# The first 128 tokens of one expert, gathered early and multiplied in float32, in a two-layer kernel with a mixture of experts

## The chip, the core and the metric

The kernel runs on one core of a Trainium2 chip, as one program with one instruction stream for each engine: PE (TensorE), DVE (VectorE), ACT (ScalarE), POOL (GpSimd) and SP (SyncE, which only starts DMAs here). The metric is device time in microseconds of one execution; the kernel before takes 1387.16 us, the median of three runs (1385.14 to 1389.26 us).

## The reference

x is (32, 64, 1024) in float32, seen as N = 2048 rows ("tokens") of 1024. There are two layers, and the change touches the second alone:

```python
x = x + L0_ffn(L0_cond(x))          # a grouped convolution, then an NF4 feed-forward with LoRA
# L1_cond: an 8-fold mixture of 64x64 kernels over the channels of each batch element
att = softmax(gelu(gelu(emb @ W0 + b0) @ W1 + b1) @ W2 + b2)
z = einsum('boi,bih->boh', einsum('bk,koi->boi', att, weight), x) + (att @ bias_k)[:, :, None]
# L1_ffn: each token goes to one of 8 experts
sel = argmax(softmax(z @ gate_w.T + gate_b))
for j in range(8):
    out = out + where(sel == j, z @ expert_w[j].T + expert_b[j], 0)
x = x + out
```

The gate's argmax decides which weights (1024 x 1024 floats an expert) a token meets. Worked out from the reference's inputs, the experts get 788, 125, 536, 196, 99, 180, 56 and 68 of the 2048 tokens, and expert 0 gets 391 of the first 1024.

## The kernel before, in words

**The first layer** takes the first 1045 us or so. It ends with the accumulators `acc` (16 tiles of 128 tokens) in SBUF.

**The mixing stage** runs over those 16 tiles (the loop at L1587). For tile t, PE mixes channels (`mixed`, L1514), ACT copies the sums out of PSUM as z32 (`mixed_out`, L757), PE transposes them (`z_transposed`, L1524), ACT copies the turned tile (`z_copied`), PE multiplies by the gate (`gate`, L1534), DVE adds the gate's bias (`logit`, L1081), PE turns the eight logits to rows (`pick_out`, L1546) and DVE copies them (`picked`). POOL stores each tile's z rows to HBM in two DMAs (L515), and SP loads expert 0's weights one eighth (`kt`, 512 KB) at a time as tiles finish (`load_expert`, L432). An SP wait on `z_ready` sets when each eighth may go.

**Placing.** The tokens are sorted by expert in tiles of 128 with no host help. `choose` makes one-hot rows of the argmax. `ranks` (PE, L1550) counts, for each token, the tokens before it that chose the same expert. `places` and `digits` (DVE) turn rank and expert into a slot. `marked` (DVE, L1132) makes two indicator rows for each tile of tokens, and `placed` (PE, L1567) multiplies them into one table in PSUM that holds at each slot the token's number. This is done in three batches of tiles, `BATCHES = (0, 6, 11, 16)`. After the last one, DVE turns the sums into `table` (L1198), then works out which expert and which column of the table each of the NS = 23 output tiles has (`etf`, `columns`, `through`, `side`, `loads`, L1201 to L1224). In the meantime PE has nothing to multiply and runs dummy products (`spin`, L1287).

**The expert stage** is 23 tiles, always all of them. For tile s:

- POOL's queue, written out by hand in `tile` (L564), gathers z rows by the table three tiles ahead (`gather_z`), gathers x rows two ahead (`gather_x`), adds the expert's bias to the x rows by a DMA one ahead (`add_bias`, semaphore `xb_in`) and scatters the finished tile.
- PE transposes the gathered z rows (`rows_transposed`, L1614, issued inside the tile before), and multiplies: 8 values of kt, two halves of 512 columns, three products each (`three`, L1279: high x high, high x low, low x high of a split of float32 in two float32r parts), so 48 products of 128 x 512.
- ACT makes the high parts (`convert_high`, with `z_high`), DVE the low parts (`convert_low`, with `z_low`), from the raw weights `wraw` for every tile anew. There is one copy of the split weights (`whr`, `wlr`), so that kt of the next tile is converted once PE has done kt of this one.
- DVE adds the product to the x rows (`add_rows`, L1246), at the end of the conversion of the next tile, and waits for `xb_in` before it.

The first tile has its own code: `first_high` on ACT (all eight high parts, then the turned z in halves), `first_low` on DVE, and `rows_transposed(0, 0)` and five more `spin` products on PE.

Of the kernel before, what the change touches and what calls it, by code (L numbers as in the profile page):

```python
# [48 lines left out]
BATCHES = (0, 6, 11, TILES)  # L49
# [41 lines left out]
def program(nc, x_nat, x_conv, toep, cond_t, ctx_w_t, chan_bias, codes_up, codes_dn, am_up, am_dn, bias_up,  # L91
# [5 lines left out]
    with ctx:  # L97
# [3 lines left out]
        def sb(stack, name, shape, dt=F32):  # L101
# [134 lines left out]
        columns = sb(moe, "columns", [P, NSP], I32)  # L236
# [3 lines left out]
        eti = sb(moe, "eti", [P, NSP], I32)  # L240
        side = sb(moe, "side", [P, NSP], I32)
        sidef = sb(moe, "sidef", [P, NSP])
        loaded = sb(moe, "loaded", [P, 2, NSP])
        loads = sb(moe, "loads", [P, 2, NSP], I32)
# [3 lines left out]
        xidx = sb(moe, "xidx", [P, 4], I32)  # L248
        xg = sb(moe, "xg", [P, 4, L])
        zg = sb(moe, "zg", [P, 4, L])  # L250
# [34 lines left out]
            "iotas", "route_const", "route_dve", "chosen", "seen_ready", "rank_mm", "total_mm", "row_ready", "slot_mm"))  # L285
        table_ready, columns_ready, tiles_ready = sem("table_ready"), sem("columns_ready"), sem("tiles_ready")
        half_turned, half_high, half_low = sem("half_turned"), sem("half_high"), sem("half_low")
# [17 lines left out]
        def gate_bank(t):  # L305
            return bank[{TILES - 3: 0, TILES - 2: 1, TILES - 1: 4}.get(t, 6)]
# [18 lines left out]
        def _(sp):  # L325
# [118 lines left out]

            for kt in range(KT):
                sp.sem_inc(wraw_in[1][kt], 16)
            load_expert(0)
            load_expert(1)
# [6 lines left out]
        def _(pool):  # L455
            last_row = pool.to_reg(N - 1)
# [55 lines left out]
            for t in range(TILES):  # L512
                pool.wait_ge(z_ready, 2 * (t + 1))
# [10 lines left out]
            def gather_z(i, s):  # L524
# [4 lines left out]
                if isinstance(i, int) and 4 * i + s == 0:  # L529
                    rows = table[:, 0:1]  # L530
# [60 lines left out]
        def _(act):  # L591
# [190 lines left out]
            def first_high():  # L782

                for kt in range(KT):
                    act.wait_ge(wraw_in[0][kt], 16)
                    nc.scalar.activation(whr[:, kt], wraw[:, 0, kt], ACT.Copy).then_inc(whr_ready, 1)
                both = pair[2][:].rearrange("p (k s) -> p k s", k=KT)
                act.wait_ge(half_turned, 1)
                nc.scalar.activation(zth[:, 0, 0:KT // 2], both[:, 0:KT // 2], ACT.Copy).then_inc(half_high, 1)
                act.wait_ge(tr_mm, 1)  # L790
                nc.scalar.activation(zth[:, 0, KT // 2:], both[:, KT // 2:], ACT.Copy).then_inc(zth_ready, 1)
# [22 lines left out]
            first_high()  # L814
            act.wait_ge(tiles_ready, TABLES)
            for i in rounds(act, NS // 4):
                for s in range(4):
                    if not (isinstance(i, int) and i == s == 0):
# [5 lines left out]
        def _(dve):  # L824
# [289 lines left out]

            def places(b):
# [8 lines left out]
            def digits(b):  # L1124
                a, z = BATCHES[b:b + 2]
                link(nc.vector.tensor_copy(sloti[:, 0, a:z], slotf[:, a:z]))
                nc.vector.tensor_single_scalar(sloti[:, 1, a:z], sloti[:, 0, a:z], P - 1, ALU.bitwise_and).then_inc(route_dve, 1)
                step[0] += 1
# [9 lines left out]
            for t in range(TILES):  # L1138
# [4 lines left out]
                if t == TILES - 1:  # L1143
                    marked(6, 7)
# [11 lines left out]
                elif t == 2:  # L1156
                    nc.vector.tensor_scalar(far[:], iota_f[:, 0:E], float(N), None, ALU.mult).then_inc(route_const, 1)
# [8 lines left out]
                elif t == 7:  # L1166
                    choose(0)
                elif t == 8:
                    places(0)
                    digits(0)  # L1170
                elif t == 9:
                    count_seen(0)
                    marked(0, 2)
                elif t in (10, 11):
                    marked(2 * t - 18, 2 * t - 16)
                elif t == 12:
                    choose(1)
                    count_seen(1)
                elif t == 13:
                    places(1)  # L1180
                elif t == 14:
                    digits(1)
            logit(TILES - 1)
            picked(TILES - 2)
            marked(7, 8)
# [4 lines left out]
            digits(2)  # L1190
            marked(10, TILES)

            dve.wait_ge(total_mm, 1)
            link(nc.vector.tensor_tensor(more[:], by_entry(bank[1][:, 0:E], TILES),
                                         room[:].rearrange("p (o e) -> p o e", o=1).broadcast_to([P, E, TILES]), ALU.is_gt))
# [13 lines left out]
            link(nc.vector.scalar_tensor_tensor(out=columnf[:], in0=etf[:], scalar=float(TILES), in1=iota_f[:, 0:NSP],  # L1209
                                                op0=ALU.mult, op1=ALU.add))  # L1210
            link(nc.vector.tensor_tensor(columnf[:], columnf[:], begin[:], ALU.subtract))
            nc.vector.tensor_copy(columns[:], columnf[:]).then_inc(columns_ready, 1)
            nc.vector.tensor_scalar(through[:], start[:], float(KT), 1.0, ALU.mult, ALU.add).then_inc(tiles_ready, 1)
            nc.vector.tensor_copy(eti[:], etf[:]).then_inc(tiles_ready, 1)
            dve.wait_ge(tiles_ready, 2)
            nc.vector.tensor_single_scalar(side[:], eti[:], 1, ALU.bitwise_and).then_inc(tiles_ready, 1)
            dve.wait_ge(tiles_ready, 3)
            nc.vector.tensor_copy(sidef[:], side[:]).then_inc(tiles_ready, 1)
# [4 lines left out]
            for b in range(2):  # L1223
                nc.vector.tensor_scalar(loads[:, b], loaded[:, b], 8.0, 16.0, ALU.mult, ALU.add).then_inc(tiles_ready, 1)  # L1224

            def first_low():
                both = pair[2][:].rearrange("p (k s) -> p k s", k=KT)
                for kt in range(KT):
                    dve.wait_ge(whr_ready, kt + 1)
                    nc.vector.tensor_tensor(wlr[:, kt], wraw[:, 0, kt], whr[:, kt], ALU.subtract).then_inc(wlr_ready, 1)  # L1230
                    if kt == 1:
                        for h in range(2):
                            k = slice(h * KT // 2, (h + 1) * KT // 2)
                            if h == 0:
                                dve.wait_ge(half_high, 1)
                            else:
                                dve.wait_ge(zth_ready, 1)
                            nc.vector.tensor_tensor(ztl[:, 0, k], both[:, k], zth[:, 0, k],
                                                    ALU.subtract).then_inc(ztl_ready if h else half_low, 1)
# [5 lines left out]

            def add_rows(i, s):  # L1246
                wait(dve, chunk_mm, i * 32 + KT * (s + 1))
                dve.wait_ge(xb_in[s % 4], i * 16 + 16 * (s // 4 + 1))
                nc.vector.tensor_tensor(xg[:, s % 4], xg[:, s % 4], pair[s % 2][:], ALU.add).then_inc(y_ready, 1)
# [14 lines left out]
            dve.sem_inc(wlr_ready, KT)  # L1264
            first_low()
            dve.wait_ge(tiles_ready, TABLES)
            for i in rounds(dve, NS // 4):
                for s in range(4):
                    if not (isinstance(i, int) and i == s == 0):
# [6 lines left out]
        def _(pe):  # L1276
# [257 lines left out]
            def gate(t):  # L1534
                pe.wait_ge(zt_high, t + 1)
                wait(pe, zt_ready, t + 1 - HALVED)
                if t < TILES - 3:
                    wait(pe, lt_ready, t)
                    wait(pe, logit_ready, t)
# [27 lines left out]
            def placed(first, last):  # L1567
                for t in range(first, last):
                    pe.wait_ge(row_ready, 2 * (t + 1))
                    ins = mm(bank[7][:, P:P + SC], atrow[:, t], atcol[:, t], start=t == 0, stop=t == TILES - 1)  # L1570
                if last == TILES:
                    ins.then_inc(slot_mm, 1)
# [14 lines left out]
            for t in range(TILES + 2):  # L1587
                if t < TILES:
                    z_transposed(t)
                if 1 < t < TILES:  # L1590
# [5 lines left out]
                elif t == 8:  # L1596
                    ranks(0)
                elif t == 13:
                    ranks(1)
# [12 lines left out]
            pe.wait_ge(table_ready, 1)  # L1612
# [9 lines left out]

            def product(i, s):
                first = isinstance(i, int) and i == s == 0
                if first:
                    pe.wait_ge(half_low, 1)
                else:
                    pe.wait_ge(ztl_ready, i * 4 + s + 1)

                wait(pe, y_ready, i * 4 + s - 1)  # L1630
                for kt in range(KT):
                    if first and kt == KT // 2:
                        pe.wait_ge(ztl_ready, 1)
                    pe.wait_ge(wlr_ready, i * 32 + KT * (s + 1) + kt + 1)
                    for h in range(2):
                        d = slice(h * 512, (h + 1) * 512)
                        ins = three(bank[2 * (s % 2) + h], zth[:, s % 2, kt], ztl[:, s % 2, kt], whr[:, kt, d],
# [6 lines left out]
            spin(bank[1], 5)  # L1644
            for i in rounds(pe, NS // 4):
                for s in range(4):
                    product(i, s)
# [69 lines left out]
```

## Time and profile before

| | us |
|---|---|
| three runs, median (lowest to highest) | 1387.16 (1385.14 to 1389.26) |
| the profiled execution's own time | 1384.71 |
| its span in the trace | 1383.1 |
| mixing stage, first `mixed` to last `gate` | 1045.2 to 1090.8 |
| first expert product starts | 1106.51 |
| last `add_rows` starts | 1378.3 |

The span is what the trace shows between the first and the last instruction; the execution's own time has 1.6 us around it. PE is busy for 99% of the span, but its spins count as busy. DVE is busy for 81% of the span, and for nearly all of the expert stage. Times below are from the span's start.

### The profile page before, as it was taken

How to read it: one execution, taken by the hardware profiler on the slowest of the kernel's cores; microseconds unless marked ns; L12 is line 12 of the kernel's file. 1: busy time of each engine (PE TensorE's matmuls, PEld its weight loads, DVE VectorE, ACT ScalarE, POOL GpSimd, SP SyncE). 2: the span in 40 equal slices, each digit the busy share in tenths (PEclk: the TensorE clock that was granted, in tenths of full speed). 3: DMA queues.
4: the chain of work that ended last, by engine and by line, in shares of the span. 5: the costliest groups of instructions: out<-in, count | busy, mean ns of one | idle time of the engine just before them, and what ended most of it. 6: DMA issues, size and time to landing. Idle time of an engine off the chain costs nothing.

```text
span 1383.1 us, 20668 instructions
## 1 busy us (share of the span) xinstructions
PE 1369.2 (99%) x6816; PEld 1125.6 (81%) x6816; DVE 1113.5 (81%) x1127; ACT 774.5 (56%) x872; POOL 225.6 (16%) x251
## 2 busy tenths in 40 slices
PE   9999999999999999999999999999999899999998
PEld 8987888888888888888888888888765688888887
DVE  7879887878878788787887887878643799999997
ACT  6665554545454545445464554555216677777774
POOL 0120000001000000000000000000013256645653
PEclk9999999999999999999999999999999999999999
DMA  7863756587874779666886759885588786978952
GB/s 243 343 248 137 270 205 244 188 290 250 276 272 176 273 252 288 238 241 225 282 250 245 261 195 298 255 286 214 198 303 283 238 256 153 375 198 290 352 173 54
DMA packets 105108, 339.50 MB, mean 245 GB/s; under 512 B 15716, under 2 KB 23404, under 8 KB 105036
## 3 DMA queue, kind: packets, MB, share of 16 engines
q1 hardware_dynamic: 79122, 257.93, 50.1%
q0 software_dynamic: 25376, 80.24, 21.5%
q8 instruction: 36, 0.59, 0.2%
q10 hardware_dynamic: 546, 0.50, 0.1%
q14 instruction: 28, 0.23, 0.0%
HBM read 303.49 MB, written 46.14 MB: 253 GB/s over the span
## 4 chain that ended last, share of the span: by engine, by line
PE 94%; DVE 3%; issue 1%; ACT 1%; DMA 0%; POOL 0%; DVEq 0%; SPq 0%; ACTq 0%; POOLq 0%
PE pair L1281 27%; PE pair L1282 27%; PE pair L1283 27%; PE pair L1350 4%; PE pair L1618 1%; DVE wf L873 1%; PE pair L1530 1%; PE pair L1520 1%; PE pair L1464 1%; PE pair L1382 1%; PE pair L1365 1%; PE pair L1542 1%; PE pair L1343 1%; PE pair L1290 1%; PE pair L1419 0%
## 5 line engine op out<-in xcount | busy, mean ns | idle before, releaser
L873 DVE TENSOR_TENSOR wf<-wf,term 128x1024 f32<-128x1024 f32 x308 | 376.5, 1222 | 62.7 <-ACT term L618 48.3
L618 ACT ACTIVATE term<-codes 128x1024 f32<-128x1024 int32 x308 | 320.6, 1055 | 137.7 <-DVE wf L873 137.7
L1281 PE MATMUL pair<-wh,hh 128*128 128x512 f32 x672 | 263.3, 392 | 1.6 <-DVE acc L937 1.3
L1282 PE MATMUL pair<-wl,hh 128*128 128x512 f32 x672 | 262.0, 390 | 0.0
L1283 PE MATMUL pair<-wh,hl 128*128 128x512 f32 x672 | 262.0, 390 | 0.0
L1281 PE MATMUL pair<-ring,wh 128*128 128x512 f32 x624 | 242.9, 389 | 0.0
L1282 PE MATMUL pair<-ring,wh 128*128 128x512 f32 x624 | 242.9, 389 | 0.0
L1283 PE MATMUL pair<-ring,wl 128*128 128x512 f32 x624 | 242.7, 389 | 0.0
L943 DVE TENSOR_TENSOR acc<-acc,pair 128x1024 f32<-128x1024 f32 x160 | 194.5, 1216 | 46.2 <-PE pair L1283 40.2
L807 ACT ACTIVATE whr<-wraw 128x1024 fp32r x176 | 181.1, 1057 | 63.9 <-PE pair L1283 49.8
L1255 DVE TENSOR_TENSOR wlr<-wraw,whr 128x1024 fp32r<-128x1024 f32 x176 | 203.4, 1215 | 2.1 <-ACT whr L807 1.9
L1281 PEld LDWEIGHTS pair<-wh,hh 128*128 128x128 f32 x672 | 126.2, 188 | 31.3 <-issue 2.9
L1283 PEld LDWEIGHTS pair<-wh,hl 128*128 128x128 f32 x672 | 126.1, 188 | 26.6
L1282 PEld LDWEIGHTS pair<-wl,hh 128*128 128x128 f32 x672 | 126.2, 188 | 25.9
L1281 PE MATMUL pair<-whr,zth 128*128 128x512 f32 x368 | 145.4, 395 | 0.9 <-DVE ztl L1243 0.9
L1283 PE MATMUL pair<-whr,ztl 128*128 128x512 f32 x368 | 143.5, 390 | 0.0
L1282 PE MATMUL pair<-wlr,zth 128*128 128x512 f32 x368 | 143.4, 390 | 0.0
L647 ACT ACTIVATE wh<-wf 128x1024 fp32r<-128x1024 f32 x44 | 45.6, 1058 | 174.6 <-DVE wf L892 159.8
L1283 PEld LDWEIGHTS pair<-ring,wl 128*128 128x128 f32 x624 | 117.1, 188 | 24.4
L1281 PEld LDWEIGHTS pair<-ring,wh 128*128 128x128 f32 x624 | 117.2, 188 | 24.1
L1282 PEld LDWEIGHTS pair<-ring,wh 128*128 128x128 f32 x624 | 117.2, 188 | 23.9
L489 POOL DMA_DIRECT2D acc<-x_nat x16 | 13.9, 867 | 678.7 <-DVE acc L943 678.7
(202 smaller groups left out, 1557.3 us busy)
## 6 DMA issues: line engine op xcount, KB each, us to landing
ring<-x_parts SPq DMA_DIRECT2D x320, 512.0 KB, 6.5
wraw<-exp_w SPq DMA_DIRECT2D x64, 512.0 KB, 10.5
x_parts<-stage POOLq DMA_DIRECT2D x24, 512.0 KB, 7.0
xg<-exp_b POOLq DMA_DIRECT2D x23, 512.0 KB, 7.9
codes<-codes_up SPq DMA_DIRECT2D x22, 512.0 KB, 7.1
codes<-codes_dn SPq DMA_DIRECT2D x22, 512.0 KB, 6.8
am<-am_dn SPq DMA_DIRECT2D x22, 512.0 KB, 4.1
acc<-x_nat POOLq DMA_DIRECT2D x16, 512.0 KB, 5.5
```

Of the source, the lines that this page charges most:

```text
L489: pool.dma_start(acc[:, bass.ds(i + (CT * c - 1), 1)].rearrange("p a l -> p (a l)"), x_nat[bass.ds(i * P + (CT * c - 1) * P, P)], accum_op ...
L618: return nc.scalar.activation(out, codes[:, n % 2], ACT.Relu, scale=scale, bias=-scale * bend)
L647: nc.scalar.activation(high_part(n), whole(n), ACT.Copy).then_inc(wh_ready, 1)
L807: nc.scalar.activation(whr[:, kt], wraw[:, bass.ds(buf, 1), kt].rearrange("p a n -> p (a n)"), ACT.Copy).then_inc(whr_ready, 1)
L873: nc.vector.tensor_tensor(whole(n), whole(n), term[:, e % 2], op).then_inc(term_added, 1)
L943: nc.vector.tensor_tensor(a, a, pair[2 + j % 2][:], ALU.add).then_inc(acc_added, 1)
L1255: nc.vector.tensor_tensor(wlr[:, kt], wraw[:, bass.ds(buf, 1), kt].rearrange("p a n -> p (a n)"), whr[:, kt], ALU.subtract).then_inc(wlr_r ...
L1281: mm(ps, ah, bh, start=first, stop=False)
L1282: mm(ps, ah, bl, start=False, stop=False)
L1283: return mm(ps, al, bh, start=False, stop=last)
L1290: mm(ps[:, 0:blocks * P].rearrange("p (c n) -> p c n", n=P), ones[:].bitcast(F32R), ones[:].bitcast(F32R).rearrange("p (o n) -> p o n", o= ...
L1350: ins = mm(whole_bank[:, :, g * GC:(g + 1) * GC], xcv[h][p % 4][:, k % 2, g, d:d + P], tz[h][:, d, g], start=k == g == d == 0, stop=k > 0 ...
```

## The change

The first eight tiles of tokens (1024 of them) become batch 0 of the placing. As soon as they are counted, the kernel picks the expert with the most of them (`fullest`), loads that expert's weights a second time into the other weight buffer, and makes the expert's first 128 tokens an output tile of their own, tile 0 (the "lead"). Their rows come from a table that only the first eight tiles went into. The lead is multiplied from plain float32 weights and plain float32 turned rows, with no split: 16 products instead of 48. The placing of the remaining tiles, the last batch's ranks included, follows in PE's order behind the lead's transposes and inside the lead's product. The 22 other tiles follow as before, with one tile fewer for that expert. All `spin` products of this stage are gone.

```diff
-BATCHES = (0, 6, 11, TILES)
+BATCHES = (0, TILES // 2, 11, TILES)
@@ SP
-                        sp.wait_ge(z_ready, 2 * TILES if e else 4 * kt + 2)
+                        sp.wait_ge(*((chunk_mm, kt + 1) if e else (z_ready, min(4 * kt + 2, 26))))
+            def load_lead():
+                sp.wait_ge(lead_ready, 1)
+                first = sp.value_load(eti[0:1, 0:1], min_val=0, max_val=E - 1)
+                for kt in range(KT):
+                    sp.dma_start(wraw[:, 1, kt], exp_w[bass.ds(first, 1), :, kt].rearrange("a p n -> p (a n)")
+                                 ).then_inc(wraw_in[1][kt], 16)
             load_expert(0)
+            load_lead()
             load_expert(1)
@@ POOL
             for t in range(TILES):
+                if t == TILES - 1:
+                    for k in range(ZB):
+                        pool.wait_ge(z_stored[k], 32 * (TILES // 2) // ZB)
+                    pool.wait_ge(lead_rows_ready, 1)
+                    pool.indirect_dma_start(zg[:, 0], None, z_dram[0:N // 2], bass.IndirectOffsetOnAxis(lead_rows[:], 0), ...
                 pool.wait_ge(z_ready, 2 * (t + 1))
...
-            gather_z(0, 0)
+            gather_z(0, 1)
             pool.wait_ge(columns_ready, 1)
-            for s in range(1, 3):
-                gather_z(0, s)
+            gather_z(0, 2)
             gather_x(0, 0)
             gather_x(0, 1)
@@ ACT
-            first_high()
+            first_high(0, 2)
+            lead_turned()
+            first_high(2, KT)
+            z_high(0, 1)
@@ DVE
+            def lead():
+                counts = bank[7][:, 3 * P:3 * P + E]
+                dve.wait_ge(count_mm, 1)
+                link(nc.vector.reduce_max(most[:], counts, AX.X))
+                link(nc.vector.tensor_scalar(fullest[:], counts, most[:, 0:1], None, ALU.is_equal))
+                link(nc.vector.tensor_tensor(fullest[:], fullest[:], rising[:], ALU.mult))
+                link(nc.vector.reduce_max(mark[:], fullest[:], AX.X))
+                ... (three scalars of mark: eti[0], columns[0], leadf; then taken and far)
+            def rows_of_lead():
+                dve.wait_ge(lead_mm, 1)
+                link(nc.vector.tensor_tensor(lead_column[:], bank[7][:, 2 * P:2 * P + SC], lead_column[:], ALU.mult))
+                link(nc.vector.reduce_sum(leadf[:], lead_column[:], AX.X))
+                nc.vector.tensor_scalar(lead_rows[:], leadf[:], 1.0, -1.0, ALU.mult, ALU.add).then_inc(lead_rows_ready, 1)
             def first_low():
                 for kt in range(KT):
-                    dve.wait_ge(whr_ready, kt + 1)
+                    dve.wait_ge(whr_ready, KT + kt + 1)
                     nc.vector.tensor_tensor(wlr[:, kt], wraw[:, 0, kt], whr[:, kt], ALU.subtract).then_inc(wlr_ready, 1)
+                    if kt == 3:
+                        z_low(0, 1)
+                add_rows(0, 0)
@@ PE
             for t in range(TILES + 2):
+                if t == 10:
+                    ranks(0)
+                    counted()
...
+                if t == 13:
+                    ranks(1)
+                    placed(0, TILES // 2, 2 * P, TILES // 2)
...
-            placed(0, 8)
-            spin(bank[5], 1)
-            ranks(2)
-            totals(1)
-            spin(bank[5], 2)
-            placed(8, TILES)
-            spin(bank[5], 20)
-            pe.wait_ge(table_ready, 1)
+            def lead_product():
+                for kt in range(KT):
+                    if kt == 0:
+                        pe.wait_ge(half_copied, 1)
+                    elif kt == KT // 2:
+                        pe.wait_ge(zth_ready, 1)
+                    pe.wait_ge(wraw_in[1][kt], 16)
+                    for h in range(2):
+                        ins = mm(bank[2 + h], lead_turn[:, kt], wraw[:, 1, kt, h * 512:(h + 1) * 512],
+                                 start=kt == 0, stop=kt == KT - 1)
+                    ins.then_inc(chunk_mm, 1)
+                    if kt == 1:
+                        placed(TILES // 2, TILES)
+                    elif kt == 5:
+                        pe.wait_ge(table_ready, 1)
+                        rows_transposed(0, 1)
             rows_transposed(0, 0)
-            spin(bank[1], 5)
+            placed(0, TILES // 2)
+            ranks(2)
+            totals(1)
+            lead_product()
```

DVE's calls are moved within the loop over t: `choose(0)` and `count_seen(0)` from t = 7 and 9 to t = 9, `lead()` and `places(0)` at t = 10, `digits` and `marked(0, 2)` and `(2, 4)` at t = 11, `choose(1)`, `lead_columns()` and `marked(4, 6)` at t = 12, `marked(6, 8)` and `rows_of_lead()` at t = 13, `places(1)` at t = 14, `digits(1)` at t = 15. The gate of the last tile uses the shared PSUM bank, and `pair` halves of the expert stage swap parity.

## Rows read from the trace of the kernel before

**Rows 1.** Page, part 4: the chain that ended last, by engine.

```profile
PE 94%; DVE 3%; issue 1%; ACT 1%; DMA 0%; POOL 0%; DVEq 0%; SPq 0%; ACTq 0%; POOLq 0%
```

**Rows 2.** Windows: stretch, its us, busy by engine, PEclk, DMA share, GB/s.

```profile
1075.00:1080.00 5.00, 5.00 (x59) 3.14 (x60) 2.62 (x13) 3.90 (x6) 2.35 (x4) 1.00 0.94 306
1098.00:1100.00 2.00, 2.00 (x6) 1.61 (x6) 1.62 (x7) 0.00 (x0) 0.09 (x1) 0.50 0.03 12
1102.00:1104.00 2.00, 2.00 (x10) 1.61 (x10) 1.90 (x7) 0.00 (x0) 0.36 (x2) 1.00 0.63 231
```

**Rows 3.** Timeline of PE around the placing: start, us, engine, line, operation.

```profile
1085.59 0.65 PE L1542 MATMUL pair<-zt,gts 128*32 128x128 f32 x16
1091.67 0.61 PE L1570 MATMUL pair<-atcol,atrow 128*128 128x128 f16 x8
1106.51 0.49 PE L1281 MATMUL pair<-whr,zth 128*128 128x512 f32 x1
1118.44 0.50 PE L1281 MATMUL pair<-whr,zth 128*128 128x512 f32 x1
```

**Rows 4.** Chain of waits in the expert stage: the transposes inside two tiles.

```profile
1121.46 0.87 PE pair L1618 x8
1133.23 0.87 PE pair L1618 x8
```

**Rows 5.** Waits of the expert stage with PE as the waiting engine, all of them.

```profile
PE pair L1281 <- DVE ztl L1243: 0.9, 1, 0.9
```

**Rows 6.** Timeline of DVE.

```profile
1093.98 0.19 DVE L1119 TENSOR_TENSOR place<-pair,far 128x40 f32<-128x40 f32 x1
1098.54 0.29 DVE L1198 SCALAR_TENSOR_TENSOR table<-pair,empty 128x128 int32<-128x128 f32 x1
1102.73 2.35 DVE L1230 TENSOR_TENSOR wlr<-wraw,whr 128x1024 fp32r<-128x1024 f32 x2
1123.98 1.21 DVE L1249 TENSOR_TENSOR xg<-xg,pair 128x1024 f32<-128x1024 f32 x1
1125.11 3.48 DVE L1255 TENSOR_TENSOR wlr<-wraw,whr 128x1024 fp32r<-128x1024 f32 x3
```

**Rows 7.** Timeline of POOL behind the table.

```profile
1099.91 1.12 POOL L537 DMA_INDIRECT zg<-z_rows,table  x1 [11.68 <-issue]
1103.82 1.05 POOL L537 DMA_INDIRECT zg<-z_rows,zidx  x1 [0.96 <-POOL zidx L534]
1105.91 1.02 POOL L537 DMA_INDIRECT zg<-z_rows,zidx  x1 [0.79 <-POOL zidx L534]
1109.00 1.20 POOL L548 DMA_INDIRECT xg<-x_rows,xidx  x1 [0.79 <-POOL xidx L545]
1117.76 1.00 POOL L555 DMA_DIRECT2D xg<-exp_b  x1 [4.15 <-DMA xg<-x_rows,xidx]
```

**Rows 8.** DMA issues, one stretch each, from 1088 to 1128: KB, us to landing.

```profile
z_rows<-z POOLq DMA_DIRECT2D x1, 256.0 KB, 8.5
zg<-z_rows,table POOLq DMA_INDIRECT x1, 4.4
xg<-x_rows,xidx POOLq DMA_INDIRECT x1, 8.0
xg<-exp_b POOLq DMA_DIRECT2D x1, 512.0 KB, 5.3
xg<-x_rows,xidx POOLq DMA_INDIRECT x1, 4.4
xg<-exp_b POOLq DMA_DIRECT2D x1, 512.0 KB, 7.6
wraw<-exp_w SPq DMA_DIRECT2D x16, 512.0 KB, 6.2
```

**Rows 9.** Timeline of PE in the convolution: plain float32 products, two records each.

```profile
85.00 1.95 PE L1350 MATMUL pair<-tz,late_xcv 128*128 128x128 f32 x16
86.71 0.48 PE L1343 MATMUL pair<-ctxd,ones 128*128 128x512 f32 x1
```

More of the change, by code:

```diff
@@ L235, in program @@
         columnf = sb(moe, "columnf", [P, NSP])
-        columns = sb(moe, "columns", [P, NSP], I32)
+        columns = sb(moe, "columns", [P, NSP + 1], I32)
         past = sb(moe, "past", [P, NSP, E])
         etf = sb(moe, "etf", [P, NSP])
-        eti = sb(moe, "eti", [P, NSP], I32)
-        side = sb(moe, "side", [P, NSP], I32)
+        eti = sb(moe, "eti", [P, NSP + 1], I32)
+        side = sb(moe, "side", [P, NSP + 1], I32)
         sidef = sb(moe, "sidef", [P, NSP])
         loaded = sb(moe, "loaded", [P, 2, NSP])
-        loads = sb(moe, "loads", [P, 2, NSP], I32)
+        loads = sb(moe, "loads", [P, 2, NSP + 1], I32)
+        most = sb(moe, "most", [P, 1])
+        fullest = sb(moe, "fullest", [P, E])
+        mark = sb(moe, "mark", [P, 1])
+        taken = sb(moe, "taken", [P, E])
+        leadf = sb(moe, "leadf", [P, 1])
+        lead_column = sb(moe, "lead_column", [P, SC])
+        lead_rows = sb(moe, "lead_rows", [P, 1], I32)
+        free = sb(moe, "free", [P, E, TILES])
         through = sb(moe, "through", [P, E], I32)
@@ L528, in gather_z @@
                 rows = zidx[:, s % 4:s % 4 + 1]
-                if isinstance(i, int) and 4 * i + s == 0:
-                    rows = table[:, 0:1]
+                if isinstance(i, int) and 4 * i + s == 1:
+                    rows = table[:, 1:2]
                     pool.sem_inc(zidx_ready, 1)
@@ L817, in _ @@
                 for s in range(4):
-                    if not (isinstance(i, int) and i == s == 0):
+                    if not (isinstance(i, int) and i == 0 and s < 2):
                         convert_high(i, s)
@@ L1142, in _ @@
                     picked(t - 2)
-                if t == TILES - 1:
-                    marked(6, 7)
+                if t == 9:
+                    choose(0)
+                    count_seen(0)
+                elif t == 10:
+                    lead()
+                elif t == 11:
+                    digits(0)
+                    more_digits(0)
+                    marked(0, 2)
+                elif t == 12:
+                    choose(1)
+                    count_seen(1)
+                elif t == 13:
+                    marked(6, 8)
+                elif t == 15:
+                    digits(1)
                 if t > 0:
@@ L1223, in _ @@
             for b in range(2):
[L1224 to L1228, printed above, removed]
-                    dve.wait_ge(whr_ready, kt + 1)
[L1230 to L1239, printed above, removed]
+                nc.vector.tensor_scalar(loads[:, b, 1:], loaded[:, b], 8.0, 16.0, ALU.mult, ALU.add).then_inc(tiles_ready, 1)
             def z_low(i, s):
@@ L1262, in before_it @@
                 return (i, s - 1) if s else (i - 1, 3)
[L1264 removed]
+            dve.sem_inc(wlr_ready, 2 * KT)
+            dve.sem_inc(ztl_ready, 1)
             first_low()
@@ L1268, in _ @@
                 for s in range(4):
-                    if not (isinstance(i, int) and i == s == 0):
+                    if not (isinstance(i, int) and i == 0 and s < 2):
                         convert_low(i, s)
@@ L1565, in ranks, with placed, counted @@
                 ins.then_inc(rank_mm, 1)
-            def placed(first, last):
+            def placed(first, last, at=P, end=TILES):
                 for t in range(first, last):
                     pe.wait_ge(row_ready, 2 * (t + 1))
-                    ins = mm(bank[7][:, P:P + SC], atrow[:, t], atcol[:, t], start=t == 0, stop=t == TILES - 1)
-                if last == TILES:
-                    ins.then_inc(slot_mm, 1)
+                    ins = mm(bank[7][:, at:at + SC], atrow[:, t], atcol[:, t], start=t == 0, stop=t == end - 1)
+                if last == end:
+                    ins.then_inc(slot_mm if end == TILES else lead_mm, 1)
+            def counted():
+                pe.wait_ge(seen_ready, 1)
+                mm(bank[7][:, 3 * P:3 * P + E], ones_b[:], seen[:, 0], start=True, stop=True).then_inc(count_mm, 1)
             def totals(b):
@@ L1621, in rows_transposed @@
                 ins.then_inc(tr_mm, 1)
-            def product(i, s):
[L1624 to L1628, printed above, removed]
+            def lead_product():
+                for kt in range(KT):
+                    if kt == 0:
[12 more added lines that the diff above has]
+                        rows_transposed(0, 1)
+            def product(i, s):
+                pe.wait_ge(ztl_ready, i * 4 + s + 1)
                 wait(pe, y_ready, i * 4 + s - 1)
                 for kt in range(KT):
-                    if first and kt == KT // 2:
-                        pe.wait_ge(ztl_ready, 1)
                     pe.wait_ge(wlr_ready, i * 32 + KT * (s + 1) + kt + 1)
```

101 lines of the change are left out of this document (56 added, 45 removed).

## The prediction

> **What bounds the kernel now.** I read the page first, then the chain of waits, then the timelines of each engine over 1040 to 1130 us, and last the DMA landings there. PE is busy for nearly the whole span, and the chain that ended last is 94% PE [rows 1]: the end moves only if PE reaches the same point of its work earlier. The reader should then look for the stretch where PE's time isn't work. It is between the placing's first products at 1091.67 and the first expert product at 1106.51 [rows 3]: nearly 15 us of spins, transposes and waits. In the expert stage one tile takes PE 1133.23 - 1121.46 = 11.77 us [rows 4]. PE waits there once, for 0.9 us [rows 5]. DVE is close behind: three conversions back to back take 3.48 us where one takes 1.21, so each further one (3.48 - 1.21) / 2 = 1.135 us [rows 6], and a tile needs ten such (eight weights, the turned rows, the addition), 11.35 us. So DVE gains 0.42 us a tile on PE and can't absorb a long stall at once.
>
> **The point at which I take the balance.** Tiles 2 to 22 are the same work in both kernels, in the same order: expert 0 is the fullest of the first 1024 tokens, so the lead is its first tile and it keeps six of its seven. If tile 2's product starts d earlier, the kernel ends d earlier. Before, it started 1133.23 - (1121.46 - 1118.44) = 1130.21 [rows 3, 4]. After, it waits for three things: PE being done with tile 1, the turned rows' low part of tile 2 on DVE, and `y_ready`, the addition of tile 0.
>
> **Step 1, the lead's rows.** The lead's chain on DVE at t = 10 (some ten small operations at about 0.23 us, before the bias of tile 9's gate) makes PE wait; I estimate 0.35 us. It could be nothing or 1 us. Before, the gate of tile 12 started at 1085.59 behind `ranks(1)` (0.24 us); now it goes first: 1085.35 + 0.35 = 1085.7. It takes 0.6 us, `ranks(1)` 0.25, eight placing products 0.42 (their row's 0.61 less the tail of the last one, about 0.2) [rows 3], and DVE's three operations with the hand-over 1.0: `lead_rows_ready` at 1088.0. POOL's indirect DMA began 1.08 us behind the table's end (1098.54 + 0.29, then 1099.91) [rows 6, 7], so here at 1089.1.
>
> **Step 2, when they land.** This is the largest unknown. The same gather took 4.4 us on almost idle queues. But SP now sends the last two eighths of expert 0 and all eight of the lead from about 1078.5 on: 5 MB, while z stores go on, into a stretch whose DMA share is 0.94 at 306 GB/s [rows 2]. That backlog lasts past 1090. The last z store, which met the first four eighths of expert 1 (2 MB) right behind it, took 8.5 us [rows 8]. I take 6.2 us, the median landing of the 16 weight loads of 1040 to 1130 [rows 8]; the ends are 4.4 and 8.5. So the rows land at 1095.3 (1093.5 to 1097.6).
>
> The Trainium skill, "DMA: Bandwidth & Descriptors", section "Queues, rings and completion order", says that each DMA engine switches between the queues that have work after every packet, so a gather shares with the weights' queue and doesn't stand behind it. By that rule the gather's 0.52 MB costs its own time once more (1.7 us at the stretch's 306 GB/s), 6.1 us in all, and the sum below would end 0.1 us lower; by the z store's 8.5 us it would end 2.3 us higher.
>
> **Step 3, the table is later.** PE's order is now: the lead's transposes, `placed(0, 8)`, `ranks(2)`. So the last ranks stand behind the gather. Transposes 1.0, placing 0.42, ranks and the hand-over 0.4: `places(2)` at 1095.3 + 1.85 = 1097.2, where it was 1093.98 [rows 6]. Everything on DVE behind it moves by delta = 3.2 us (1.4 to 5.5): the table is done at 1102.0, `first_low` starts at 1105.9.
>
> **Step 4, PE's side.** A plain float32 product of 128 columns costs (86.71 - 85.00) / 8 = 0.214 us [rows 9], one of 512 four times that, 0.855; the lead has 16, so 13.7 us instead of 11.77 - 0.87 = 10.9 for 48 split ones. It starts at about 1097.1. Two values of kt 3.4, the wait for DVE's last marks (1097.7 + 3.2 = 1100.9) and `placed(8, 16)` to 1101.4, four values 6.8, the transposes of tile 1 (its gather is issued at 1103.1 and lands at 1107.5 at the earliest) to 1109.2, two values 3.4: tile 1's product can start at 1112.6, where it was 1118.44. PE's clock was at 0.50 (its lower level, 1.2 GHz) in 1098:1100 after PE had idled, and back at 1.00 by 1102:1104 [rows 2]. The new order has an idle stretch at the same place and no spins; if kt 0 and 1 run at the lower level they cost 3.4 more, of which the wait for the marks hides 0.4. I expect 1112.6 to 1115.6. With tile 1's 11.77 us PE is free for tile 2 at 1124.4 to 1127.4, so PE alone would gain 3 to 6 us.
>
> **Step 5, DVE's and POOL's side.** `first_low` is eight conversions and one of turned rows, 10.2 us: done at 1116.1. Then stands `add_rows(0, 0)`, which waits for `xb_in[0]`, the bias added by DMA to the gathered x rows. Before, this addition stood behind nine more conversions, at 1123.98, and found the data there. Queued behind it now are all of tile 2's conversions, and for these PE waits. POOL's chain: before, the x gather was issued at 1109.00 and took 8.0 us, the bias at 1117.76 and took 5.3 us, so it landed at 1123.06 [rows 7, 8]. Now one z gather fewer stands ahead of it: tile 0's is done. That takes off 1105.91 - 1103.82 = 2.1 us (the spacing of two z gathers on POOL) [rows 7]. But the table is 3.2 later: the net is +1.1. The x gather meets expert 1's weights as before (they now follow the lead's kt, some 300 GB/s in all), so I keep 8.0 and 5.3. The bias lands at 1124.2. DVE idles 8.1 us. The addition (1.135) and three conversions with the turned rows (4.54) end at 1129.9, and with 0.1 for the hand-over tile 2's product starts at 1130.0.
>
> **The sum.** 1130.21 - 1130.0 = 0.2 us gained, nothing that can be seen. The profiled execution would take 1384.71 - 0.2 = 1384.5. The median of the runs lies 2.45 above that execution: 1387.16 - 0.2 = 1387.0 us. Costed at nothing: ACT's copies of the lead's rows (ACT had converted all of expert 0 by 1097.5 and then had nothing to do until the first tile's rows); the z store of tile 15, pushed behind the gather by about 3 us (needed only at the table); expert 1's later load (not used before tile 7, 60 us later). If the first cover were gone the copies cost 1.2 us.
>
> **The rivals.**
> *Faster.* The stall of `add_rows(0, 0)` is short because POOL's chain runs on quick DMAs. For it: a later x gather (at 1123.75) landed in 4.4 us [rows 8]. Against it: the first two both took 8.0, and the same weight traffic is there. With 4.4 for it and for the lead's gather, the bias lands at 1123.06 + (1.4 - 2.1) - 3.6 = 1118.8 and tile 2 starts at 1124.6; PE's own limit is then 1122.6 to 1125.6. Gain 5.2: 1382.0 us.
> *Slower, the late lead.* The lead's gather is held up by the 5 MB of weights, and `ranks(2)` stands behind it. Each us goes into the table and so into `xb_in[0]` one for one. It decides from a landing of more than 6.4 us on (below that the kernel isn't slower), and passes 0.3% at 10.6 us. For it: the z store's 8.5 us beside only 2 MB. Against it: those 8.5 us include its own queue's stores. At 9.6 us, with the bias at 7.6 (the next bias landing) [rows 8], it costs 3.4 + 2.3 - 0.2 = 5.5: 1392.7 us.
> *Slower, the clock.* PE stays at 1.2 GHz for the whole lead: 13.7 us more, tile 1 starts at 1126.3 and tile 2 at 1138.1, 7.9 late: 1395.0 us. Against it: before, the clock came back within 6 us, under spins that kept PE busy [rows 2].
> *It doesn't do what it says.* The lead's weights arrive too late. 5 MB from 1078.5 have until 1109; that is 165 GB/s of the 306 that the stretch moves. It would look like the clock case, with less of it.
>
> **How the numbers follow.** The case above 0.60, faster 0.21, the late lead 0.12, the clock or late weights 0.07. Its own range is 1384.5 to 1390. The range for 8 in 10 takes in most of the faster case and some of the late lead: 1381.8 to 1391.4. A measurement of this kernel can tell about 0.3%, 4.2 us. Faster by more than that is the faster case and little else, 0.21; slower by more than that is a part of the two slower cases and a spread of the first, 0.16; the rest, 0.63, is within it.
>
> **What would show it.** Right: DVE idle for some 8 us before the first `add_rows`, released by the bias's DMA; PE idle 3 to 6 us before tile 2; tile 1's product starting 3 to 6 us earlier than before and tile 2's within 2 us of 1130.2; `places(2)` about 3 us later. Wrong in step 2 and 3: the lead's gather landing in under 5 or over 9 us. Wrong in step 5, and with it the prediction: the bias landing before 1120, or DVE not waiting for it.

## The result, and the profile after

The changed kernel is slower: 1391.89 us against 1387.25 us, the medians of ten runs each, with a ratio of 1.0043 and a 95% interval of 1.0029 to 1.0057. The ratio isn't the quotient of the medians: these lie 4.6 us apart, the ratio stands for 6.0 us. In a later comparison of the same two kernels the ratio was 1.0040 (1.0021 to 1.0058). So some 5 to 6 us were lost where 0.2 us of gain were forecast; the stated range ended at 1391.4. One slow execution of the kernel before in that comparison (1966 us) and one of e3 below (5801 us) are left out of the ratios. The profiled execution took 1391.39 us, its span is 1389.8 us, 6.7 us more than the span before.

The chain of waits of the changed kernel, from 1085 to 1145 us, is the best view to start with. Its columns are start, us, and what the end waited for (products left out):

```profile
1088.31 8.57 DMA zg<-z_rows,lead_rows
1096.93 1.97 PE pair L1680 x8
1098.89 0.85 PE pair L1634 x8
1100.06 4.38 PE pair L1694 x8
1104.44 0.46 PE pair L1634 x8
1105.33 0.29 DVE table L1268
...
1112.78 8.62 DMA xg<-x_rows,xidx
1121.61 0.53 issue
1122.16 7.58 DMA xg<-exp_b
1129.84 0.99 DVE xg L1312
1132.45 2.38 DVE wlr L1318 x2
1134.83 1.15 DVE ztl L1298
```

The reader should see three DMAs in it, 24.8 us together: the gather of the lead's z rows, the gather of its x rows, and the addition of its expert's bias by DMA ("the bias" from here on). In the page of the changed kernel, DMA has 3% of the chain where it had 0% [rows 1]:

```profile
PE 92%; DVE 3%; DMA 3%; issue 1%; ACT 1%; POOL 0%; POOLq 0%; DVEq 0%; SPq 0%; ACTq 0%
```

Between the first and the second DMA, the chain goes through PE: the lead's transposes (L1680), the first placing products (L1634), two values of kt of the lead (L1694), the other placing products, then the table. So the table waits for the lead. Two timelines show both ends of the loss. DVE's, answering to [rows 6]:

```profile
1099.94 0.20 DVE L1179 TENSOR_TENSOR place<-pair,far 128x40 f32<-128x40 f32 x1 [5.68 <-PE pair L1628]
1105.33 0.29 DVE L1268 SCALAR_TENSOR_TENSOR table<-pair,empty 128x128 int32<-128x128 f32 x1
1116.56 4.62 DVE L1304 TENSOR_TENSOR wlr<-wraw,whr 128x1024 fp32r<-128x1024 f32 x4
1129.84 1.22 DVE L1312 TENSOR_TENSOR xg<-xg,pair 128x1024 f32<-128x1024 f32 x1 [8.66 <-DMA xg<-exp_b]
```

And PE's, answering to [rows 3]. Tile 1 starts 1.2 us earlier than before (3 to 6 us were forecast), and then PE idles for 6.45 us in front of tile 2:

```profile
1117.20 0.79 PE L1345 MATMUL pair<-whr,zth 128*128 128x512 f32 x1
...
1136.02 0.79 PE L1345 MATMUL pair<-whr,zth 128*128 128x512 f32 x1 [6.45 <-DVE ztl L1298]
1136.61 0.63 PE L1346 MATMUL pair<-wlr,zth 128*128 128x512 f32 x1
...
1140.34 1.04 PE L1680 MATMUL pair<-ident,zg 128*128 128x128 f32 x8
```

The same transposes inside tile 2, in the kernel before:

```profile
1133.07 1.03 PE L1618 MATMUL pair<-ident,zg 128*128 128x128 f32 x8
```

POOL's timeline, answering to [rows 7]: the x gather is 3.8 us and the bias 4.4 us later.

```profile
1088.31 1.11 POOL L537 DMA_INDIRECT zg<-z_rows,lead_rows  x1 [2.86 <-DMA z_rows<-z]
1106.77 1.08 POOL L563 DMA_INDIRECT zg<-z_rows,table  x1 [16.11 <-issue]
1112.78 1.19 POOL L574 DMA_INDIRECT xg<-x_rows,xidx  x1 [0.79 <-POOL xidx L571]
1122.16 1.00 POOL L581 DMA_DIRECT2D xg<-exp_b  x1 [5.74 <-DMA xg<-x_rows,xidx]
```

The first of these lines names a z store as what POOL waited for. But the gather starts 1.0 us behind the end of DVE's `lead_rows` here (1087.30) and in e5 below (1090.49, then 1091.49), so I take the row numbers as what released it.

The transposes inside tile 2 start at 1140.34 and not at 1133.07, 7.3 us later (the chain puts the earlier ones at 1133.23 [rows 4]). From there on the tiles take 11.8 us each in both, but for a few later waits: the kernel before lost 1.2 us to them and the changed one 0.4. That leaves 6.5 of the 6.7 us by which the span is longer.

### The profile page after: what moved, and what is told of

Read it like the earlier page. It is cut to its first block, busy times and chain, and to the rows that moved or that the text cites. A ratio compares the mean times of both kernels' runs of the same rounds, so it can differ in the third digit from the quotient of the medians.

```text
span 1389.8 us, 20576 instructions
## 1 busy us (share of the span) xinstructions
PE 1366.7 (98%) x6781; PEld 1119.2 (81%) x6781; DVE 1107.1 (80%) x1131; ACT 766.4 (55%) x864; POOL 217.7 (16%) x250
## 4 chain that ended last, share of the span: by engine, by line
PE 92%; DVE 3%; DMA 3%; issue 1%; ACT 1%; POOL 0%; POOLq 0%; DVEq 0%; SPq 0%; ACTq 0%
PE pair L1345 27%; PE pair L1347 27%; PE pair L1346 27%; PE pair L1414 4%; DVE wf L905 1%; PE pair L1680 1%; PE pair L1528 1%; PE pair L1594 1%; PE pair L1584 1%; PE pair L1446 1%; PE pair L1429 1%; DMA xg<-x_rows,xidx 1%; DMA zg<-z_rows,lead_rows 1%; PE pair L1407 1%; DMA xg<-exp_b 1%
## 5 line engine op out<-in xcount | busy, mean ns | idle before, releaser
L835 ACT ACTIVATE whr<-wraw 128x1024 fp32r x168 | 172.9, 1056 | 70.1 <-PE pair L1347 60.1
L1318 DVE TENSOR_TENSOR wlr<-wraw,whr 128x1024 fp32r<-128x1024 f32 x168 | 195.0, 1216 | 4.5 <-ACT whr L835 4.1
L1345 PE MATMUL pair<-whr,zth 128*128 128x512 f32 x352 | 140.5, 399 | 6.5 <-DVE ztl L1298 6.4
L1347 PE MATMUL pair<-whr,ztl 128*128 128x512 f32 x352 | 137.8, 392 | 0.0
L1346 PE MATMUL pair<-wlr,zth 128*128 128x512 f32 x352 | 137.4, 390 | 0.0
```

Source lines behind the costliest of these rows:

```text
L835: nc.scalar.activation(whr[:, kt], wraw[:, bass.ds(buf, 1), kt].rearrange("p a n -> p (a n)"), ACT.Copy).then_inc(whr_ready, 1)
L1318: nc.vector.tensor_tensor(wlr[:, kt], wraw[:, bass.ds(buf, 1), kt].rearrange("p a n -> p (a n)"), whr[:, kt], ALU.subtract).then_inc(wlr_r ...
L1345: mm(ps, ah, bh, start=first, stop=False)
L1346: mm(ps, ah, bl, start=False, stop=False)
L1347: return mm(ps, al, bh, start=False, stop=last)
```

## The experiments

Each kernel is an edit of the changed one. Ratios are to the kernel before. "The changed kernel" in a profile's numbers is the profile above; its second profile (`after_again`, below) is named where it differs. In seven of the eight profiles with a lead its weights are sent as in the changed kernel, and the lead's z gather took 8.0 to 8.6 us in them: half a microsecond more or less in a landing means nothing.

**All the placing ahead of the lead** (e1).

```diff
-            rows_transposed(0, 0)
             placed(0, TILES // 2)
             ranks(2)
             totals(1)
+            placed(TILES // 2, TILES)
+            rows_transposed(0, 0)
             lead_product()
@@ lead_product
-                    if kt == 1:
-                        placed(TILES // 2, TILES)
-                    elif kt == 5:
+                    if kt == 5:
```

> The changed kernel with PE's order turned: the last ranks, the totals and all the placing products stand before the lead's transposes, not behind them and inside its product. My theory: the table is late (105.6 less 98.8, 6.8 us) because it stands in PE's queue behind the lead's gather and behind two values of kt of the lead; through POOL's chain that makes the bias of tile 0 late, and tile 2 with it. Then the table is back at about 1099, the bias lands about 6 us earlier, tile 2 starts at about 1130 instead of 1136.0, and the time is 6 us lower: a ratio to the kernel before of 0.999 to 1.001 instead of 1.0043. Rival, contention: the extra 4 MB of weights slow the gathers whatever PE's order is; then the bias lands only 1 to 3 us earlier and the ratio stays at 1.002 or more. Rival, the lead itself: plain float32 products at the lower clock are the price, then the order changes nothing or costs.

Measured: 1.0014 (0.9993 to 1.0034), a little above the expected 1.001. Beside the changed kernel's 1.0040 in the same comparison that is 3.6 us better by the ratios and 2.5 by the medians (1389.59 and 1392.08), but the two intervals overlap. DVE's and PE's timelines of this kernel:

```profile
1094.08 0.19 DVE L1179 TENSOR_TENSOR place<-pair,far 128x40 f32<-128x40 f32 x1
1098.77 0.29 DVE L1268 SCALAR_TENSOR_TENSOR table<-pair,empty 128x128 int32<-128x128 f32 x1
1125.15 1.22 DVE L1312 TENSOR_TENSOR xg<-xg,pair 128x1024 f32<-128x1024 f32 x1 [6.37 <-DMA xg<-exp_b]
```

```profile
1114.80 0.80 PE L1345 MATMUL pair<-whr,zth 128*128 128x512 f32 x1
1131.48 0.50 PE L1345 MATMUL pair<-whr,zth 128*128 128x512 f32 x1 [4.29 <-DVE ztl L1298]
```

The table is back at its old place (1098.77; it was 1098.54), 6.6 us ahead of the changed kernel. The addition of tile 0 is 4.7 ahead and tile 2's start 4.5. So PE's order is the larger part of the loss, and the lead itself isn't: tile 1 now starts at 1114.8, 3.6 us earlier than in the kernel before. Of the 6.6 us, 1.9 didn't arrive: the lead's x rows took 9.6 us to land and the bias 8.5, against 8.6 and 7.6 in the changed kernel (9.5 and 7.9 in its second profile). In the kernel before they took 8.0 and 5.3 [rows 8]. So even with the table in its old place the two landings cost 4.8 us more than before, PE still waits 4.29 us, and tile 2's transposes (1135.93) are 2.9 us behind the kernel before. That part fits the contention rival; no run took the traffic away from this stretch, so it isn't shown.

**The lead's x rows gathered early** (e2).

```diff
@@ gather_x
+                if isinstance(i, int) and i == s == 0:
+                    nc.gpsimd.tensor_copy(xidx[:, 0:1], lead_rows[:]).then_inc(xidx_ready, 1)
@@ POOL, before the stage
+            pool.wait_ge(pick_mm, TILES)
+            gather_x(0, 0)
+            pool.wait_ge(table_ready, 1)
             gather_z(0, 1)
             pool.wait_ge(columns_ready, 1)
             gather_z(0, 2)
-            gather_x(0, 0)
+            add_bias(0, 0)
             gather_x(0, 1)
             pool.wait_ge(tiles_ready, TABLES)
-            add_bias(0, 0)
```

> The changed kernel with the lead's x rows gathered by the lead's own row numbers before the table is there, and its bias added right behind the z gather of tile 2. My theory: PE waited 6.45 us before tile 2 only because the addition of tile 0 waited 8.66 us for its bias at 1129.8. With the bias issued at about 1113 and landed by 1121, the addition starts at about 1121.2 (DVE free) or at the landing, PE finishes tile 1 at 1129 without a wait and the clock doesn't fall: tile 2 starts at about 1129, 7 us earlier, ratio 0.998 to 1.000. Rival: DVE and ACT are late anyhow (the table is 6.8 late), then tile 2 starts no earlier than about 1134 and the ratio stays above 1.002.

```profile
1100.63 1.10 POOL L576 DMA_INDIRECT xg<-x_rows,xidx  x1 [0.95 <-POOL xidx L570]
1111.71 1.00 POOL L583 DMA_DIRECT2D xg<-exp_b  x1 [0.27 <-issue]
```

```profile
1122.72 1.22 DVE L1316 TENSOR_TENSOR xg<-xg,pair 128x1024 f32<-128x1024 f32 x1 [2.79 <-DMA xg<-exp_b]
```

```profile
1128.53 0.50 PE L1349 MATMUL pair<-whr,zth 128*128 128x512 f32 x1 [0.22 <-DVE ztl L1302]
```

The table stays 6.5 us late here, and yet tile 2 starts at 1128.53, 7.5 us ahead of the changed kernel and 1.7 ahead of the kernel before. So `xb_in[0]` alone turned the late table into a late tile 2. The ratio was 1.0014 (0.9997 to 1.0032), above what I had expected: tile 2 is ahead of the kernel before and the whole isn't. In this profile 5.1 us were lost again later (see the head start, below).

**The lead's weights held back** (e4).

```diff
                 for kt in range(KT):
+                    if kt == 2:
+                        sp.wait_ge(zg_in[0], 16)
                     sp.dma_start(wraw[:, 1, kt], exp_w[bass.ds(first, 1), :, kt]...
```

> The changed kernel with the lead's weights held back from the third eighth on until the lead's z rows have landed: 3 MB fewer in SP's queue while the gather runs. If the 8.6 us of that gather are contention with the weights, it lands in 4.4 to 6 us, the last ranks start 2.5 to 4 us earlier, and the kernel gains 2 to 4 us on the changed one (ratio 1.0015 to 1.003), unless the lead then waits for its weights. If the gather is slow for another reason (its own queue's z stores), it still takes 8 us and the ratio stays at 1.004 or rises.

Measured: 1.0018 (0.9999 to 1.0036). The DMA view gives the landing of the lead's gather, from its start, in the changed kernel and then here:

```profile
zg<-z_rows,lead_rows POOLq DMA_INDIRECT x1, 8.6
```

```profile
zg<-z_rows,lead_rows POOLq DMA_INDIRECT x1, 6.4
```

With 3 MB fewer in SP's queue the gather lands 2.2 us sooner, the table is done 2.8 us sooner (1102.55), and tile 2's transposes come at 1137.07, 3.3 us sooner. The ratio is 3.1 us below the changed kernel's 1.0040, again with overlapping intervals. Against the 8.0 to 8.6 us of the profiles without this edit, these 3 MB cost the gather 1.6 to 2.2 us. What takes the other 2.0 us beyond the 4.4 of a gather on idle queues [rows 8], the weights still in the queue or the z stores in the gather's own, no run separates.

**Dummy products in the wait** (e5).

```diff
+            spin(bank[5], 22)
             rows_transposed(0, 0)
             placed(0, TILES // 2)
```

> The changed kernel with 22 dummy products in PE's queue while it waits for the lead's rows (4.7 us of the 5.1 us wait at the upper level). If the fall of the granted clock to 0.50 in 1094 to 1102 is part of the price, the clock stays at 1.00, the transposes and placing take 1.9 us instead of 3.0 and the first two kt of the lead 3.4 instead of 4.5: the table is 2 us earlier and the kernel gains about 2 us (ratio 1.003). If the clock doesn't matter, or is hidden, the ratio stays at 1.004.

Measured: 1.0045 (1.0026 to 1.0063), the same as the changed kernel. In this profile the mixing stage begins 3.2 us later (1048.16 instead of 1044.97), before anything that the edit touches. Counted from the start of the last gate, the first two kt of the lead took 3.5 us instead of 4.4, and the table was done 2.3 us earlier. Of that, 2.1 us are the transposes, the placing and the two kt, the rest the gather. Tile 2's start came 2.2 us earlier, but its transposes only 1.2, as PE's clock stayed at its lower level longer in tile 2 (it did so in the second profile of the changed kernel too). Nothing of that shows in the ratio, and whether the 3.2 us belong to the kernel or to this execution isn't known. The clock's first fall thus costs about 2 us of the table; whether it costs the end anything stays open.

**Both** (e3), the edits of e1 and e2 in one.

> Both earlier edits in one: all placing products ahead of the lead's transposes, and the lead's x rows gathered by the lead's own row numbers. My theory: with the table back at 1099 and the bias of tile 0 no longer last, only PE decides when tile 2 starts: tile 1 at 1114.8 as with the placing first, so tile 2 at 1126.6 to 1127.5, 3 us ahead of the kernel before, and 9 ahead of the changed one. Ratio 0.997 to 0.999, if the later waits for bias DMAs (1.2 us in the kernel before, 5.0 and 4.3 in the profiles of the two single edits) don't eat it. Rival: those later waits are the balance of a stage in which DVE has no slack, so that any head start at tile 2 is lost within the 21 tiles; then the ratio is 1.000 to 1.002.

Measured: 0.9990 (0.9971 to 1.0009), the edge of what was expected, and clearly below the changed kernel's 1.0040. In its profile, no wait of PE is left in the expert stage, and the bias isn't waited for at all:

```profile
1115.59 4.62 DVE L1308 TENSOR_TENSOR wlr<-wraw,whr 128x1024 fp32r<-128x1024 f32 x4
1120.12 1.21 DVE L1316 TENSOR_TENSOR xg<-xg,pair 128x1024 f32<-128x1024 f32 x1
1121.26 3.49 DVE L1322 TENSOR_TENSOR wlr<-wraw,whr 128x1024 fp32r<-128x1024 f32 x3
```

Tile 2's transposes are at 1131.15, 1.9 us ahead of the kernel before, and its span is 1380.3 us, 2.8 less. This profile is of one of the fastest executions (1381.91 us; the median is 1386.32, that of the kernel before 1387.71). The head start is smaller than the 3 us expected because the clock stayed at its lower level until about 1103:

```profile
1094.00:1096.00 2.00, 0.59 (x8) 0.22 (x5) 1.76 (x11) 0.00 (x0) 0.00 (x0) 0.50 1.04 422
1102.00:1104.00 2.00, 2.00 (x4) 0.89 (x3) 1.86 (x10) 2.00 (x3) 1.13 (x2) 0.54 0.73 209
```

In e1, with the same order on PE, it was back by about 1101, and the first twelve products of the lead took 11.2 us instead of 12.4. So the moment at which the clock comes back can differ with the same order on PE.

**Both, with nine dummy products** (e9).

```diff
             placed(0, TILES // 2)
+            spin(bank[5], 4)
             ranks(2)
             totals(1)
+            spin(bank[5], 5)
             placed(TILES // 2, TILES)
             rows_transposed(0, 0)
```

> The same with four dummy products behind the first eight placing products and five behind the totals, in PE's idle stretches while DVE marks the last rows. If the granted clock stays at 1.00, the lead's transposes take 1.0 us instead of 1.9 and its first twelve products 10.3 instead of 11.2: tile 1 and tile 2 start 1.8 us earlier than without them, ratio 0.996 to 0.998. If it falls all the same, no difference.

Measured: 0.9959 (0.9943 to 0.9975), 1382.98 us in the median of seven: the best of all, and faster than both the kernel before and the changed one. My expectation for the clock was wrong in one point. It didn't stay at 1.00; it fell later and came back sooner, and the transposes still took 1.9 us:

```profile
1096.00:1098.00 2.00, 1.15 (x5) 0.48 (x5) 2.00 (x12) 0.00 (x0) 0.00 (x0) 1.00 1.03 420
1098.00:1100.00 2.00, 1.90 (x10) 1.67 (x10) 1.60 (x8) 0.60 (x1) 0.18 (x1) 0.51 0.89 363
1102.00:1104.00 2.00, 2.00 (x6) 0.95 (x5) 1.86 (x9) 2.00 (x3) 1.78 (x2) 1.00 0.64 147
```

Tile 2's transposes are at 1129.94, 1.2 us ahead of e3 and 3.1 ahead of the kernel before. But the first twelve products of the lead took 11.3 us, and e1 had 11.2 without any dummy product: these profiles don't show that the dummies made the 1.2 us. The two ratios differ by more (0.3%, with intervals that barely touch). That e9 is faster than the kernel before is measured; what sets it apart from e3 isn't shown.

**The changed kernel again.**

> The changed kernel unaltered, beside the others on one chip. The loss should show again, ratio 1.003 to 1.006, with the first addition of the expert stage waiting 7 to 10 us for its bias and PE about 5 to 7 us before tile 2. If its ratio were near 1.001, the earlier edits would not have gained what I read from them.

Measured: 1.0040 (1.0021 to 1.0058); the addition waited 9.36 us, PE 7.15 us before tile 2. The lead's gather took 8.1 us, its x rows 9.5, its bias 7.9, and tile 2's transposes came at 1142.37, 9.3 us behind the kernel before.

**The head start and what eats it.** In most profiles DVE now and then waits for a bias of a later tile: five times in e2, four times in the kernel before, once in the changed one, and not at all in its second profile, in e5 and in e3. Not every such wait reaches PE. The largest is in e1, with PE's wait six microseconds later:

```profile
1283.58 1.22 DVE L1312 TENSOR_TENSOR xg<-xg,pair 128x1024 f32<-128x1024 f32 x1 [5.71 <-DMA xg<-exp_b]
```

```profile
1289.47 0.49 PE L1345 MATMUL pair<-whr,zth 128*128 128x512 f32 x1 [2.46 <-DVE ztl L1298]
```

From the spacing of the tiles (11.8 us without a wait), PE lost 1.2 us after tile 2 in the kernel before, 0.4 in the changed one, 5.2 in e1, 5.1 in e2, 2.8 in e4, 5.0 in e9 and nothing in e3 or in the second profile of the changed kernel. So e1, e2 and e9, in which tile 2 starts well ahead of the changed kernel, lost some 5 us again, but e3, which starts as early, lost nothing. It may be that these waits eat a part of a head start. One profile each doesn't say whether the differences belong to the kernels or to the single executions. The runs of one kernel spread over 5 us and more (1387.4 to 1396.77 for the changed one), so a good part belongs to executions.

## Why the prediction was wrong

**What held.** Steps 1 and 5 as mechanisms: `lead_rows_ready` came at 1087.3 (1088.0 forecast). DVE idled 8.66 us in front of the first addition, released by the bias's DMA (8.1 forecast). PE idled 6.45 us in front of tile 2 (3 to 6 forecast). The start of tile 2 was set by that addition. e2 shows it: only POOL's order was changed, with the lead's x rows and bias ahead, and of PE's wait 0.22 us were left. The float32 product cost what step 4 said: four of 512 columns in 3.6 us with the tail of the last, 0.86 us each.

**What failed is the size of terms: of the lead's gather (step 2), of the table's delay behind it (step 3) and of the landings behind the table (step 5).** The time was to be the same because POOL's chain lost 3.2 us by the late table, won 2.1 by the missing gather, and PE had room. Measured, the chain lost 6.8 by the table and 2.9 by slower landings and won 3.0, so the bias landed 6.7 us later than before where 1.1 were forecast. One by one:

- Step 2, the lead's gather: 6.2 us taken, 8.6 measured. It was issued 0.8 earlier, so it landed 1.6 later. This is the value of the z store's row [rows 8], which I had as an end and not as the estimate. e4 shows that some 2 us of it are contention with the lead's own weights. The Trainium skill, "DMA: Bandwidth & Descriptors", section "Queues, rings and completion order", lets engines alternate between queues after each packet; my estimate from it was 6.1 us, and the trace doesn't agree with the estimate: 8.6 us beside the backlog, 6.4 beside a smaller one. It doesn't speak against the rule: from 1088 to 1097 POOL's queue had 39% of the engines' time and SP's 62%. But POOL's queue moved 1.41 MB in it, and the gather is only 0.52 of that. The rest is traffic of its own queue, the z stores above all, which the estimate left out.
- Step 3, the table: 3.2 us later forecast, 6.8 measured. 1.6 are the landing. 1.15 are the stretch from the transposes to the last ranks, 3.0 us instead of 1.85, with the granted clock at 0.50. The last 0.85 are the step's own omission: I took DVE's marks as the last thing in front of the placing products, but the two kt of the lead at the lower clock ended after them. Step 4 had this delay and didn't carry it into the table. e1 gives the whole 6.6 back by order alone.
- Step 4, tile 1: 1112.6 to 1115.6 forecast, 1117.20 measured. The lead's product started 3 us later than forecast, and PE waited 1.44 us inside it for tile 1's z rows, which come by the late table. PE was done with tile 1 at 1129.6, so even without the wait nearly nothing was gained.
- Step 5, the landings behind the table: the x gather 8.6 instead of 8.0, the bias 7.6 instead of 5.3. Together with the table (which came through POOL as 3.8 instead of 1.1; the missing gather took off 3.0 and not 2.1, a term that erred the other way) the bias landed at 1129.8 and not at 1124.2. From there DVE took 6.2 us instead of 5.8, so tile 2's product started at 1136.0 and not at 1130.0. The 5.3 us came from a stretch with other traffic than I assumed: while that bias was under way in the kernel before, SP's queue moved 0.05 MB and POOL's 0.92; in the changed kernel they moved 0.67 and 1.25. Expert 1's weights now go out one by one behind the products of the lead, up to 1118.12, where before the last had gone out by 1110.80. So "as before" didn't hold for the bias. That this made it slower is argued, not shown.
- A cost that no step had: PE's wait in front of tile 2 brought the clock down a second time. Six steps between products of tile 2 were 0.43 us instead of 0.23, and the first was longer too: 4.3 us from its start to its transposes, where e2, without a wait, took 2.9. That is 1.4 us (2.4 in the second profile). I priced the lower clock only at the lead, where most of it is hidden.

The measured time is within 1 us of the late-lead rival's 1392.7 us, which had a chance of 0.12. That rival had the mechanism (the ranks behind the gather, one for one into `xb_in[0]`) and the 7.6 us of the bias. What it lacked was the knowledge that these weren't mishaps but the rows nearest to the case: both stood in the list. That its time fits to 1 us is in part luck. It had a landing of 9.6 us where 8.6 were measured, and neither the clock in front of the table nor the second fall.

**A limit of the balance point.** The prediction took tile 2's start as the end's measure. In e2 tile 2 starts 1.7 us ahead of the kernel before, and its ratio is 1.0014: a head start at tile 2 isn't handed on whole.

**Where the gain of the change was.** It is small: with the placing first and the x rows early, tile 2 is 1.9 to 3.1 us ahead. The kernel is 0.4% faster than before in e9; in e3 the interval includes no change. In the changed kernel as written, the gain was turned into a wait for a DMA chain that starts at the table.

## What to carry to other kernels

When work is pulled into an idle stretch, look at what stands behind it in the same queue: here the last ranks and the placing, the start of everyone's next chain, were put behind a gather of 8.6 us. An early result is worth only as much as its latest companion; the lead's product was early, its x rows and bias weren't, although their row numbers were known at the same moment. And for a DMA that meets a backlog which the change itself makes, take the landing from the row that met such a backlog, not from the median.

## What the runs showed of the hardware

- Gathers of the same 512 KB: 4.4 us on idle queues [rows 8], 6.4 with the smaller backlog of e4 in SP's queue, 8.0 to 8.6 with that of the changed kernel, where the DMA share was 1.01 to 1.03 at 408 to 418 GB/s from 1092 to 1098. In e2 and e3 the lead's x gather, issued at about 1100.6 when that backlog was gone, took 4.4 us.
- The granted clock fell from 1.00 to 0.50 after PE had been idle from 1091.8, and again in PE's wait of 6.45 us. In the second case it came back 3 us after the products had started, and more than 5 us after them in the second profile of the same kernel. With nine dummy products in the first stretch (e9) it was still 1.00 in 1096 to 1098, where e3 had 0.50, and then fell all the same.
